# Value products of six attention layers: four matmuls of 32 output rows in place of two of 64

## The reference

```python
def shift_tokens(t):                     # second half of the features comes from the token before
    a, s = jnp.split(t, 2, -1)
    s = jnp.pad(s, ((0, 0), (1, 0), (0, 0)))[:, :-1]
    return jnp.concatenate([a, s], -1)

def attn_layer(x, Wqkv, qs, ksc, Wo):    # 16 heads of 64, windows of 32 tokens
    qkv = x @ Wqkv
    q, k, v = jnp.split(qkv, 3, -1)      # then split into heads
    ...
    q = l2norm(q) * qs
    k = l2norm(k) * ksc
    ...                                  # rotary factors on q and k
    out = local_attention(q, k, v)       # softmax over this window and the one before
    return out.transpose(0, 2, 1, 3).reshape(b, n, INNER) @ Wo
```

## Time and profile before

| what | value |
|---|---|
| median of 3 runs | 4652.31 us (4650.04 to 4658.37) |
| the profiled execution: its own time | 4656.79 us |
| its span, first to last instruction | 4655.0 us |
| mean granted TensorE clock over the span | 0.935 |
| busy: PE, DVE, ACT, POOL | 4112.3, 3561.9, 2988.6, 2212.4 us |
| PE, L832 (values) | 828.5 us in 3072 records |
| PE, L864 and L888 (scores, mix) | 415.1 and 824.6 us in 24576 records |
| ACT, L1303 (copy of values) | 457.0 us, 768 times |

### The profile page before, as it was taken

How to read it: one execution, slowest core, us unless ns; L and a number is a source line. 1 busy time by engine, 2 the same in 40 slices (tenths; PEclk the granted TensorE clock), 3 DMA queues, 4 the chain that set the end, 5 groups by cost and what they waited for, 6 DMA issues and landing times. The chain is left out here.

```text
span 4655.0 us, 112822 instructions
## 1 busy us (share of the span) xinstructions
PE 4112.3 (88%) x40172; PEld 2362.1 (51%) x40175; DVE 3561.9 (77%) x8496; ACT 2988.6 (64%) x5496; POOL 2212.4 (48%) x1392
## 2 busy tenths in 40 slices
PE   8969999999999999999999999999999953747635
PEld 5644555555555555555555555555555532635533
DVE  7878888888888888888888888888888846356441
ACT  3427777777777777777777777777777745645302
POOL 0006665665656656566566656656565500140006
PEclk9989999999999999999999999999999975868557
DMA  1013222322223222232222322223222200000202
GB/s 41 1 54 67 62 58 62 80 59 61 60 60 81 63 59 60 58 82 65 59 59 60 76 65 63 57 64 75 64 60 61 58 17 12 1 1 6 82 9 35
DMA packets 187828, 246.44 MB, mean 53 GB/s; under 512 B 88677, under 2 KB 129383, under 8 KB 187367
## 3 DMA queue, kind: packets, MB, share of 16 engines
q1 hardware_dynamic: 182054, 240.47, 22.2%
q0 software_dynamic: 5632, 4.33, 0.7%
HBM read 41.65 MB, written 14.30 MB: 12 GB/s over the span
## 5 line engine op out<-in xcount | busy, mean ns | idle before, releaser
L1234 POOL TENSOR_TENSOR f_rot_a<-f_rot_a,f_norm 128x1024 f32<-128x1024 f32 x384 | 730.4, 1902 | 996.1 <-DVE f_norm L1073 963.6
L1226 POOL TENSOR_TENSOR f_rot_a<-f_rot_a,f_rot_b 128x1024 f32<-128x1024 f32 x384 | 908.5, 2366 | 246.3 <-issue 213.6
L832 PE MATMUL f_bank<-f_w_vo,f_xs_t 128*64 128x512 f32 x3072 | 828.5, 617 | 24.5 <-ACT f_vo L1303 24.5
L1303 ACT ACTIVATE f_vo<-f_bank 128x512 f32<-128x512 f32 x768 | 457.0, 595 | 395.9 <-PE f_bank L832 385.9
L1294 ACT ACTIVATE f_squares<-f_bank 128x512 f32<-128x512 f32 x768 | 456.4, 594 | 295.5 <-PE f_bank L819 215.6
L1052 DVE TENSOR_TENSOR f_rot_a<-f_bank,f_rot 128x512 f32<-128x512 f32 x768 | 525.0, 684 | 83.4 <-DVE f_stat L1101 42.3
L1055 DVE TENSOR_TENSOR f_rot_b<-f_bank,f_rot 128x512 f32<-128x512 f32 x768 | 516.8, 673 | 0.0
L864 PEld LDWEIGHTS f_bank<-f_k_t,f_q_t 128*32 128x32 f32 x12288 | 313.6, 109 | 315.4 <-issue 162.4
L1059 DVE TENSOR_REDUCE f_sums<-f_squares 128x16 f32<-128x1024 f32 x384 | 464.9, 1211 | 1.6
L1315 ACT ACTIVATE f_k_t<-f_bank 64x512 f32<-64x512 f32 x768 | 449.2, 585 | 4.8 <-PE f_bank L854 0.3
L1240 POOL TENSOR_TENSOR f_prob<-f_score,f_stat 128x512 f32<-128x512 f32 x384 | 400.4, 1043 | 98.6 <-DVE f_stat L1105 98.6
(11 more groups left out here) (445 smaller groups left out, 7235.4 us busy)
## 6 DMA issues: line engine op xcount, KB each, us to landing
f_vo_off<-f_vo SPq DMA_DIRECT2D x1152, 128.0 KB, 2.3
f_vo_off<-f_vo SPq DMA_DIRECT2D x384, 64.0 KB, 2.0
f_w_qk<-in_Wqk SPq DMA_DIRECT2D x12, 512.0 KB, 5.9
f_vo_dram<-f_vo_pair SPq DMA_DIRECT2D x48, 128.0 KB, 1.8
f_x_shifted<-s_all SPq DMA_DIRECT2D x48, 128.0 KB
f_x_shifted<-s_all SPq DMA_DIRECT2D x48, 127.0 KB
f_w_vo<-f_vo_dram SPq DMA_DIRECT2D x10, 512.0 KB, 4.0
e_w<-in_e_W SPq DMA_DIRECT2D x2, 2048.0 KB, 12.1
```

The costliest lines, as they stand in the source:

```text
L832: done = nc.tensor.matmul(bank[V][64 * n:64 * n + 64, :], x, w_vo[:, 4 * g:4 * g + 4, n, :], start=True, stop=True)
L1226: nc.gpsimd.tensor_tensor(rot_a[:, slot, :, :], rot_a[:, slot, :, :], rot_b[:, g, :, :], ALU.add).then_inc(rot_summed, 1)
L1234: nc.gpsimd.tensor_tensor(heads, heads, over(norm[:, 16 * g:16 * g + 16], [128, 16, HEAD_DIM]), ALU.mult).then_inc(qk_normed, 1)
L1303: nc.scalar.activation(vo[:, g, 2 * (t % 2) + j, :], flat(V), ACT.Copy).then_inc((va_copied, vb_copied)[j], 1)
```

## The change

`values` makes each call's result by four matmuls of 32 tokens in place of two of 64. Matmul w writes partitions 32w to 32w + 31 of the same bank, from tokens 32 (w mod 2) of the call's 64 and the half n = w // 2 of `w_vo`. The bank holds the same numbers at the same places afterwards; the order of the groups, the semaphores, ACT's copies and the DMAs stay.

```diff
                 x = chunk_x(t)[:, 64 * j:64 * j + 64]
-                for n in range(2):
-                    done = nc.tensor.matmul(bank[V][64 * n:64 * n + 64, :], x, w_vo[:, 4 * g:4 * g + 4, n, :], start=True, stop=True)
+                for w in range(4):
+                    at = 32 * (w % 2)
+                    done = nc.tensor.matmul(bank[V][32 * w:32 * w + 32, :], x[:, at:at + 32], w_vo[:, 4 * g:4 * g + 4, w // 2, :], start=True, stop=True)
                 return done
```

## The result

The changed kernel takes 4786.17 us (median of 4 runs, 4783.23 to 4794.28) against 4653.63 us for the kernel before: a ratio of 1.0287, 95% interval 1.0269 to 1.0305. It is 132 us slower, where 63 us of gain were forecast.

What follows compares the result with a forecast made beforehand. PE was taken as the bound, busy 69.1 of 70.7 us a pass; gains of 1.32 us a pass x 47.5 = 63 us gave 4594, adjusted to 4590 us. Own range 4570 to 4605; 8 in 10, 4545 to 4622.

Steps and rivals of the forecast that it cites:

- part (4): What replaces the saved PE time: waits for ACT and DVE cut each quarter's 0.58 us; no DMA or queue affected.
- part (5): Total over the layers: 1.32 us a pass, times 47.5 passes, 63 us gained, hence 4590 us.
- parts (1) and (2): In values: four matmuls of 32 keep a pass at 0.43 us, and doubled weight loads run under matmuls; cost 0 each.
- PE is the bound, and width changes cost time: In the layers PE is busy 69.1 of 70.7 us a pass; each array width change costs some 0.15 us more.
- the 70.3: Sign of being wrong: a pass of the layers over 70.3 us.
- The sum: Gains per pass, quarters 0 to 3 and remaining value calls: 0.26 + 0.40 + 0.16 + 0.40 + 0.1 = 1.32 us.
- The new wait for ACT's copy: Quarters 1 and 3, ahead of the second values call: PE waits 0.18 us for ACT, leaving 0.40 us gain each.
- Quarter 2 is ACT's: ACT works through to 2074.37, where PE waits 0.59 us; only 0.16 us of quarter 2's gain counts.
- Loads open: Slower rival in values: serial weight loads add 0.34 us a call, 134 us in all, 4786 us; chance 0.05.
- DVE holds quarters 3 and 0: Rival: DVE gives only its 0.25 us there, so 0.9 us a pass, 43 us, 4609 us; chance 0.20.
- The rule against the change: Skill's rule: weight loads overlap matmuls only in different row groups, so values' doubled loads would stand open and lose.
- A granted clock under 1.00: Sign of being wrong: granted clock below 1.00, the 2.4 GHz level, in the layers.

Runs made afterwards that it cites:

- run 5: The changed kernel with 160 satisfied PE waits ahead of the loop, shifting where its body begins: 4598.76 us, ratio 0.9878 to the kernel before.
- run 13: The kernel before with four matmuls of 32 only in the g = 1 value calls, and 56 satisfied waits right ahead of the loop: 4649.63 us, ratio 0.9989.
- run 6: The kernel before, its values untouched, with 224 satisfied PE waits ahead of the loop: 4671.13 us, ratio 1.0034.
- run 7: The kernel before with four matmuls of 32 only in the g = 0 value calls, and 128 satisfied PE waits ahead of the loop: 4592.03 us, ratio 0.9867.

## Why the prediction was wrong

**The step that failed** is the end of part (4), "No DMA is moved and no queue is passed", and with it the sum in part (5), which has no term for fetching instructions: it put that at nothing without a reason. The cost 0 of parts (1) and (2) held: four matmuls of 32 and their loads take PE no longer. But I priced them on the array, and by what they hold up on ACT and DVE, and never counted them as instructions that PE must have at hand. The change adds 128 to a loop body of 1593; its body touches an eighth packet, and each turn fetches all of it again, at 4.3 us a pass against a gain of 1.4. The row was there: the page of the kernel before names an instruction queue with 59 packets, 0.97 MB, and that is PE's whole program once, so the loop fetched nothing. A question to that line (how near is the body to what stays?) would have made a rival.

What it cost: with its instructions at hand (run 5) a pass takes 69.32 us, without them 73.64, so 4.32 us more. Of these 3.3 us are the wait at the turn (145.7 us in the 44 turns). The other 1.0 is the clock: where it falls it costs some 1.7 us (the values behind the turn start 3.58 us after it, 2074.70 to 2078.28, and 1.88 after it in the kernel before, 2084.41 to 2086.29), and it falls behind 26 of 44 turns. PE's busy time says the same: 68.3 us a pass against 67.3 in run 5. Times 44 turns the loss is 190 us, the gain of 1.41 us a pass 62 us; the difference, 128 us, is nearly all of the 132 measured.

The Trainium skill has this (Runtime: NRT & Kernel Launch, Instruction fetch mechanics): PE's instruction memory holds 128 KiB, 2048 instructions, filled in blocks of 16 KiB, and a taken branch to a block that isn't there stalls PE until it is fetched. The trace agrees on the block (16384 bytes) and on the stall. The Trainium skill's window of two blocks does not agree: a body across seven stays (59 to 61 packets in all). Eight blocks would be the 2048, and seven of the body with one fetched ahead would fill them. That reading fits every row of the table, and it fits the 9 packets that a turn fetches where the body touches 8; but no run shows the block ahead by itself, and the soft edge stays open.

**Point by point.**
- *PE is the bound, and width changes cost time*: right. A pass with its instructions at hand takes 69.32 us, where I had written 69.4, and run 13 shows that the gain hangs on the neighbours' width. The pass of 73.64 us without them is over the 70.3 that I had named as a sign of being wrong.
- *The sum*, of what it covers: 1.32 us a pass forecast, 1.41 measured (70.73 less 69.32, run 5). From the first start of mix to the projection the run of five went from 5.05 to 4.73 us in quarter 0, to 4.61 in quarter 1 and to 4.52 in quarter 2, and from 5.10 to 4.63 in quarter 3: gains of 0.32, 0.44 and 0.47 where I had 0.26, 0.40 and 0.40. Of quarter 2's 0.53 the wait for ACT takes back 0.4. I had priced ACT's round trip 0.04 to 0.07 us too long.
- *The new wait for ACT's copy*: right in kind. In quarter 0 the copy is also ahead of scores: seed ends, scores start at 2004.62, 0.95 us after values and not 0.86, which I had not listed.
- *Quarter 2 is ACT's*: right, but the wait does not grow at seed (0.6 us as before). It grows one group earlier, at values in quarter 3: 0.9 us in place of 0.5.
- *Loads open*, the slower rival: wrong. The doubled loads cost nothing that shows. Its working had a slip besides: a pass has 16 value calls, not 8, so the kept gain is 0.08 us a call, and the rival should have read 0.26 x 768 = 200 us, some 4850.
- *DVE holds quarters 3 and 0*: it did not. Its 0.99 us for ACT shrank to 0.60, as forecast, and was not used up.
- *The rule against the change* (the Trainium skill's, on loads and row groups): the runs decide against it here, for loads of 32 columns beside each other: eight loads a call, and values take no longer.
- *A granted clock under 1.00* was named as a sign that would make the prediction wrong. It did come, only behind waits at the turn.

The 4590 us were thus the time of a kernel with its instructions at hand; such kernels measured 4592 to 4599. As a forecast of this change it was wrong in sign.

## What to carry to other kernels

Count instructions as a resource of their own: ahead of any change that adds some to a loop's body, read the instruction queue's packets on the page, and how many packets of 256 the body touches; where the queue is silent while the loop runs, more instructions in it, or merely code ahead of it, can end that. If a changed loop shows a wait for "issue" at its turn, shift the body's start before giving the change up: here that alone turned 1.0287 into 0.9878. And groups of matmuls of one width next to each other are worth making alike: in quarter 2 of run 5 the run of five is 0.53 us shorter with four width changes gone, 0.13 us each.

## What the runs showed that I had not expected

- Code that runs once and does nothing, ahead of a loop, made a kernel whose loop was untouched 8.5% slower (5052 against 4658 us), and 24 instructions more of it (run 6) cost 0.3%.
- The edge is not sharp: with the body's end 3 to 26 instructions inside the eighth packet 2 of 44 turns were lost, with 35 to 58 inside 43 of 44.
- The loss depends on the place too: 3.3 us of waiting a turn for the changed kernel, 6.8 us for the kernel before shifted by 200.
- The granted clock did not fall behind every wait at the turn: behind 26 of 44 in the changed kernel (waits of 3.3 us on average), behind all 44 in the kernel before shifted by 200 (6.8 us).
- A nop without a wait leaves no instruction on PE; a satisfied wait does. Ahead of the loop 224 of them cost 15 us, 0.07 us each; 128 of them (run 7) cost less apiece, as the loop starts only 3 us later.
